# A fused attention and FFN layer on one core: one stack load split around the maxima of unit 2, and the last unit's PV in two sessions

## What is computed

```python
xn = layernorm(x)
q, k, v = split(xn @ w_qkv.T + b_qkv)          # 16 heads of 16 channels
att = q @ k.T / 4 + bias(pos_independent)      # bias: features of query position times features of key position
att = softmax(where(causal, att, -inf))
y = (att @ v) @ w_proj.T + b_proj
f = fp8_gemm(bf16(xn), kernel) + bias_f        # both operands rounded to fp8 values
out = x + y + f
```

## Time and profile before

| | |
|---|---|
| median of 3 runs | 822.24 us (822.04 to 825.26) |
| the profiled execution | 820.26 us |
| its span in the trace | 818.5 us |
| mean granted TensorE clock | 0.973 of full speed |
| PE busy | 747.2 us, 91% of the span |
| DVE, ACT, POOL busy | 628.9, 581.0, 528.2 us |
| q1, the queue that carries SP's DMAs | 102.96 MB, 60.4% of 16 engines |

### The profile page before, as it was taken

One profiled execution on the slowest core, in us unless ns is written; L12 is line 12 of the kernel. 1 busy time (PEld: TensorE's weight loads), 2 busy tenths in 40 slices (PEclk: granted clock), 3 DMA queues, 4 the chain that ended last, 5 costly groups with the idle time before them and its releaser, 6 DMA issues.

```text
span 818.5 us, 23154 instructions
## 1 busy us (share of the span) xinstructions
PE 747.2 (91%) x6313; PEld 510.0 (62%) x6313; DVE 628.9 (77%) x2395; ACT 581.0 (71%) x1258; POOL 528.2 (65%) x525
## 2 busy tenths in 40 slices
PE   6869999999999999999999999999999999999883
PEld 3546666666676667657676666657666666767552
DVE  3767878887977878788788878787787879778722
ACT  4236767777786877778687777778677777867671
POOL 6433568567666867667676757766685776667580
PEclk8859999999999999999999999999999999999998
DMA  6834666567566656666566657756665775666502
GB/s 170 165 68 95 114 145 123 129 148 144 127 138 153 118 130 138 138 145 137 141 121 151 123 127 162 142 126 137 148 117 123 155 143 124 139 130 121 120 24 86
DMA packets 55548, 106.07 MB, mean 130 GB/s; under 512 B 10464, under 2 KB 30432, under 8 KB 55520
## 3 DMA queue, kind: packets, MB, share of 16 engines
q1 hardware_dynamic: 53192, 102.96, 60.4%
q10 hardware_dynamic: 2328, 2.77, 1.0%
HBM read 18.68 MB, written 8.91 MB: 34 GB/s over the span
## 4 chain that ended last, share of the span: by engine, by line
PE 49%; ACT 15%; SPq 11%; issue 9%; DMA 7%; DVE 5%; ACTq 3%; DVEq 1%; POOL 0%; POOLq 0%
SPq L328 11%; PE misc_a L539 8%; PE misc_a L655 8%; PE scoreT_b L629 6%; PE misc_b L539 6%; ACT probs L911 6%; PE scoreT_a L629 3%; DMA stacks<-neg_max_T 3%; PE misc_b L655 3%; PE score_a L606 3%; PE score_c L606 2%; ACT qk_parts L818 2%; ACT out_T L884 2%; ACT attn_hi L893 2%; ACT xnT_hi L807 1%
## 5 line engine op out<-in xcount | busy, mean ns | idle before, releaser
L1187 POOL TENSOR_SCALAR_AFFINE_SELECT probs<-probs 128x512 f32<-128x512 f32 x256 | 159.5, 635 | 244.7 <-ACT probs L911 242.8
L989 DVE CUSTOM_DVE_ANT_0 score_b<-score_b,causal_mask_q 128x384 f32<-128x384 f32 (+3 forms) x321 | 161.9, 521 | 119.6 <-PE score_b L606 118.4
L989 DVE CUSTOM_DVE_ANT_0 score_a<-score_a,causal_mask_q 128x512 f32<-128x512 f32 x319 | 173.1, 559 | 8.1 <-PE score_a L606 4.1
L911 ACT ACTIVATE probs<-scoreT_b 128x384 f32<-128x384 f32 (+1 forms) x256 | 134.5, 525 | 60.7 <-issue 23.7
L989 DVE CUSTOM_DVE_ANT_0 score_c<-score_c,causal_mask_q 128x256 f32<-128x256 f32 (+3 forms) x384 | 171.4, 474 | 2.3 <-PE score_c L606 2.2
L911 ACT ACTIVATE probs<-scoreT_a 128x512 f32<-128x512 f32 (+1 forms) x256 | 145.6, 569 | 14.0 <-PE scoreT_a L632 7.4
L989 DVE DVE_READ_ACCUMULATOR2_ANT row_max<- 128x1 f32 x1024 | 142.9, 140 | 0.0
L911 ACT ACTIVATE probs<-scoreT_c 128x384 f32<-128x384 f32 (+1 forms) x256 | 136.2, 532 | 3.7 <-PE scoreT_c L632 3.3
L655 PE MATMUL misc_a<-probs,v_ones 128*32 128x128 f32 (+3 forms) x1536 | 131.2, 438 | 0.4 <-POOL probs L1187 0.4
L629 PE MATMUL scoreT_a<-stacks 64*128 64x512 f32 (+3 forms) x320 | 108.3, 358 | 21.8 <-DMA stacks<-neg_max_T 13.8
L629 PE MATMUL scoreT_b<-stacks 64*128 64x384 f32 (+3 forms) x320 | 119.5, 393 | 7.6 <-ACT probs L911 7.1
(11 more groups left out here) (241 smaller groups left out, 1948.9 us busy)
## 6 DMA issues: line engine op xcount, KB each, us to landing
stacks<-qk_parts SPq DMA_DIRECT2D x128, 512.0 KB, 8.1
x_ring<-in_L_attn_x SPq DMA_DIRECT2D x16, 512.0 KB, 3.6
xn<-recips SPq DMA_DIRECT2D x31, 256.0 KB
out<-x_ring SPq DMA_DIRECT2D x15, 512.0 KB, 3.0
attn<-out_T SPq DMA_DIRECT2D x48, 128.0 KB, 2.6
stacks<-neg_max_T SPq DMA_DIRECT2D x128, 4.0 KB
attn<-out_T ACTq DMA_DIRECT2D x16, 128.0 KB, 2.9
low_features<-neg_max_T SPq DMA_DIRECT2D x124, 4.0 KB
```

Of the source, the lines that this page charges most:

```text
L911: A(probs_slot(g, k), STB[(SLOTS * g + k) % 3][:, 0:w], ACT.Exp).then_inc(exp_done, 1)
L989: last = V.tensor_tensor_reduce(bank, bank, CMQ[:, T - w:T], 1.0, LEAST, ALU.add, ALU.max, MX[:, g % 2, 8 * h + 4 + qt:8 * h + 5 + qt])
L1187: last = GP.affine_select(out=d, in_=d, compare_op=ALU.is_ge, fill=0.0, base=0, pattern=[[0, HU], [1, P]], channel_multiplier=-1)
```

## The change

Three things are changed. PV of unit 3 is done in two sessions: key tile 0 after slot (0, 0), and `job_MT` with key tiles 1 to 3 after (0, 3). `T_lo(1)` is moved from (0, 0) to (3, 11), and the inversion of the denominators from (0, 8) to (0, 7). `load_stack(b + 1, 0)` is issued as one DMA before `load_max(b, 2)` and one behind it. In the last body, where no stack is loaded, the third doesn't apply; in the first, the first two don't apply to the PV (there is none before it).

```diff
-PV_AT = [(1, 0), (2, 3), (3, 3), (0, 3)]
+PV_AT = [(1, 0), (2, 3), (3, 3), (0, 0)]
 
-PV_REST_AT = {0: (1, 3)}
+PV_REST_AT = {0: (1, 3), 3: (0, 3)}
...
-XL_AT, FIRST_XL_AT = [(3, 10), (0, 0)], [(0, 3), (0, 3)]
+XL_AT, FIRST_XL_AT = [(3, 10), (3, 11)], [(0, 3), (0, 3)]
 
-INVERT_AT, LAST_INVERT_AT = (0, 8), (3, 8)
+INVERT_AT, LAST_INVERT_AT = (0, 7), (3, 8)
...
-            def load_stack(b, g):
+            def load_stack(b, g, pairs=(0, 1)):
 
-                for u in (2 * g, 2 * g + 1):
+                for u in (2 * g + i for i in pairs):
                     r = 32 * (u % 4)
                     sp.dma_start(STK[:, u, :, :].bitcast(F32), QKP[r:r + 32, u // 4, :, :, :].bitcast(F32)) \
                         .then_inc(stack_loaded[g], 16)
...
                 if not last:
                     wait_alone(sp, (w_loaded, 16), (st_ready, ROW * b + SLOTS),
                                (ql_ready, 4 * (b + 1) + 2))
-                    load_stack(b + 1, 0)
+                    load_stack(b + 1, 0, (0,))
                 load_max(b, 2)
+                if not last:
+                    load_stack(b + 1, 0, (1,))
                 regroup(b, 0, first)
```

## The result

The changed kernel takes 878.76 us (median of 4 runs, 876.42 to 883.57), against 823.75 us before (median of 4): a ratio of 1.0667, 95% interval 1.0604 to 1.073. That is 55 us slower. The forecast was 849.0 us in a range of 812 to 872, so the sign and the first step were right and the size was not.

A forecast was written before the change was run, and what follows sets the result against it. PE, busy 91% of the span, was taken to bound the kernel. The profiled 820.26 us plus 26.7 for the second stack DMA, other moves 0, made 847.0; 1.98 more to the median gave 849.0, range 812 to 872.

The forecast's parts named there:

- the sign: Whole kernel: slower, with chance 0.77 in all, against 0.11 for no difference and 0.12 for faster.
- the first step: Slot (2, 0): the second pair is late by more than the maxima were, chance 0.71, +26.7 us.
- The second stack DMA and its stall: Slot (2, 0): issued at +3.06 us, landing 6.8 us later, PE stalls 2.70 against 0.92 us; +1.78 a body, +26.7 us.
- The clock: Rival, chance 0.06: stalls of 2.7 us in slot (2, 0) halve PE's clock, 2.5 us lost a body, 886 us.
- The first stack DMA and the maxima: Slot (2, 0): with one stack DMA ahead, PE's 0.92 us wait for the maxima goes, a gain of 13.8 us.
- The inversion at (0, 7): Inversion 0.6 us earlier, making the first stack DMA earlier, which nobody waits for: 0, at worst +0.3 us a body.
- PV in two sessions and `T_lo(1)`: Slots (0, 0) and (3, 11): idle 0.58 us for the exp becomes 0.58 us for `T_lo(0)`; both moves worth 0.
- What stands behind on SP: SP's queue: unit 0's regrouping goes earlier than now, unit 1's stack not later than now; no effect.
- The port rule: Second stack DMA: 32 partitions at some 218 GB/s plus 2 us fixed, landing after 4.4 us, gaining 0.6 a body.

The follow-up runs named there:

- the filled run: Changed kernel with 10 bf16 matmuls of 512 columns put before PE's wait for the stack in slot (2, 0): 853.96 us, ratio 1.0412.
- the repaired version: Changed kernel with unit 0's chunks reordered so the second pair is first read, and waited for, in slot (2, 6): 819.51 us, ratio 0.9927.
- the other moves alone: Changed kernel with the stack load whole again, so only PV of unit 3, `T_lo(1)` and the inversion are moved: 819.84 us, ratio 0.9968.
- the split alone: Kernel before with only the stack load of unit 0 split around the maxima: 886.47 us, ratio 1.0756.

## Why the prediction was wrong

*The second stack DMA and its stall* were right. The prediction had 2.70 us in (2, 0) of each of 15 bodies; the trace has 2.81. The second pair was issued 3.50 us behind the first issue of the maxima (mean of 15, 2.6 to 4.6; 3.06 was taken), the lone DMA 6.6 to 6.8 (6.8 was taken). The size of that transfer was right, its reason only in part. What stands behind a transfer was said not to slow it, from the earlier trace rows and the line of six; but the first stack DMA, with its twin taken away from behind it, lands after 6.6 us at the mean in place of 7.3. The 6.8 that was taken came from another place, beside unit 3, and that it fits a lone DMA so well is partly luck. With the stalls alone the kernel takes 853.96 us, as the filled run shows, inside the forecast's own range of 830 to 872.

*The clock* was the step that failed: the sum has nothing for it. The prediction had it as a rival with 0.06 and priced it at 2.5 us a body (886 us). Against it stood "idle times of up to 1.6 us don't do it now", and that was carried over to 2.7 us, where no row of the trace stood. The fall came in 13 of 15 bodies and costs 1.81 us a body, 25 us in all. Of the 55 us it makes nearly half. The start of the program, had the right warning: 2.0 us of idle time out of 6 before a fall. The Trainium skill, page "TensorE: Matmul & The Clock Gate", part 1, has the clock set by a monitor of how busy PE has been of late; the trace agrees in kind (1.00 before the stall, 0.5 behind it), and the filled run shows that in these stalls it is PE's own idleness that brings the clock down.

*The first stack DMA and the maxima.* The wait for the maxima did go, 13.8 us to 0.8. But the prediction took all 0.92 us a body for PE's gain, and did not ask what is late next: the FFN's bank, 0.42 us a body. In the change itself this lay hidden in the longer stall. By the waits, this is what keeps the repaired version from the 13.8 us: of the 12.6 us of waits that went, 6.3 came back at the bank. Against the kernel before, a body of it is 0.27 us shorter, and against the other moves alone it is no shorter, so the order was worth at most that.

*The inversion at (0, 7)* was priced at nothing, "the first stack DMA earlier, which nobody waits for". In the change as it is that is nearly so in its words and wrong in its effect. The stall of the split alone is 3.5 us in a body (52.5 us in 15), that of the whole change 2.81, and the timelines of SP show where the 0.7 us come from: with the split alone the first stack DMA goes out 1.56 us ahead of the maxima and the second pair 4.21 us behind their first issue (mean of 15), in the whole change 2.2 us ahead and 3.50 us behind. With the stack whole it takes the waits for the maxima from 13.8 us to 4.2. What was feared for it, a wait for the denominators, stayed at 1.1 us in one body of 15 (it was 0.6).

*PV in two sessions and `T_lo(1)`* were right: 0, an idle time of 0.59 us for `T_lo(0)` in the place of 0.58 us for the exp. *What stands behind on SP* was right as well: no wait for the regrouping appears. The stack of unit 1 did go out later, 2.4 us behind the end of slot (1, 11) where it was 1.4, in the bodies shown, and nothing waited for it.

*The port rule* that was weighed, 4.4 us for 32 partitions (page "SBUF — State Buffer" of the Trainium skill, "Door 1: The DMA port swizzle" and the setup-cost knee), is not borne out here: 6.6 to 6.8 us for a transfer with next to nothing beside it. The measurement decides. Which side of the transfer limits it was not tried.

## What to carry to other kernels

When a step is moved behind a wait, add the whole time from issue to landing to the moment when the wait ends, and compare with the first use, not with the average: here 4.1 us were left for 6.8. Price a new stall of PE twice, once by its length and once by what the clock does afterwards, and take no comfort from shorter idle times that were harmless. And before a wait is taken for a gain, look for the wait right behind it in the same slot; here it took back half of what the DMA's wait had given up.

## What the runs showed of the hardware

The granted clock stays at 0.50 for 3.4 or 6.8 us behind such a stall, though PE is busy again for all or most of it; how long it takes to come back doesn't follow the length of the stall (6.8 us behind 2.17 us idle at 126.9, 3.4 us behind 4.00 us at 487.3). Nor does it take a stall: at the beginning of the last body of the run with 10 filling matmuls the clock fell at 787 us, with PE busy 7.63 of the 8 us before:

```profile
779.00:787.00 8.00, 7.63 (x75) 5.24 (x67) 6.45 (x27) 5.00 (x12) 4.54 (x5) 1.00 0.69 165
787.50:790.50 3.00, 3.00 (x16) 1.30 (x9) 1.57 (x7) 0.63 (x2) 3.00 (x3) 0.50 0.94 130
```

What brought it down there no run shows.

A DMA of 4 KB took SP as little as 0.6 us to issue, and up to 3.1 us behind two DMAs of 512 KB in the kernel before. Beside unit 1 the four issues took 2.6 to 4.6 us behind one stack DMA (the changed kernel) and 4.9 to 7.7 behind two (the kernel before). So the issue itself, and not only the transfer, gets longer while earlier transfers are under way; that it waits for room in the queue is an inference that no run tested.
